# The triangle contraction taken by output side, with the moments, the next weight fold and the first normalization moved inside it, and contraction and finish in one block

## The chip, the cores and the metric

One core of one Trainium2 chip. The metric is device time in microseconds; the median of three runs is compared. The profile is one execution of the whole program.

## The reference

Four residual layers are applied in turn to an image `x` of 256 x 256 tokens with 64 channels. Each layer is a group normalization of x, followed by a "triangle multiplication":

```python
def layer(x):                       # x: (256, 256, 64), float32; weights differ per layer
    z  = layernorm(groupnorm(x))    # statistics of groupnorm run over the whole image
    a  = (z @ Wa + ba) * sigmoid(z @ Wag + bag)      # layers 0 and 2: also * mask
    b  = (z @ Wb + bb) * sigmoid(z @ Wbg + bbg)
    o  = einsum('ikc,jkc->ijc', a, b)                # layers 1 and 3: 'kic,kjc->ijc'
    g  = sigmoid(z @ Wog + bog)
    return x + ((layernorm(o) * g) @ Wo + bo         # layers 0 and 1: gate first
                if gate_first else (layernorm(o) @ Wo + bo) * g)   # layers 2 and 3
```

Layer 0 rounds a and b to bfloat16 before the contraction; the other layers contract in float32.

## The kernel before

Each layer runs through the same stages, one after the other.

- `prepare`: a few tiny operations that turn the statistics of x into the group normalization. It is a block of its own (a block ends with a barrier of all engines).
- One block with `norm` (x is normalized, split into two float16 parts and stored to DRAM as XH or XHA), and then, for each half of the channels, `project` (the four projections and gates, into the SBUF tensor LR) and `contract` (32 channel matrices of 256 x 256). `moments` closes this block.
- `finish`: a block of its own. It loads the contraction's result O, the normalized x (XH) and x itself (XT), and computes layer normalization, gate, output projection and residual.

**The contraction** of one half is 16 steps e; a step is four channels, eight float32 matmuls of 128 x 256 (each in two instructions), into one of four pairs of PSUM banks. Four steps are a *piece*: piece = (channel quarter cq, output side ut), with `cq, ut = divmod(piece, 2)`. So both output sides (rows 0 to 127 and 128 to 255 of the result) become complete only with the last pieces. ACT copies a step from PSUM to `obuf` (L879) and squares it (L885). DVE adds copy and squares into running sums `sum1`, `sum2` (four adds, L903 and L911). SP stores each piece to the DRAM tensor OS (OSL, in bfloat16, in layer 0); a store is 2 MB, 1 MB in layer 0.

**Moments** come after the last sum: DVE folds the two parts of the sums (L987 to L996), ACT takes logarithm and exponential (L1006, L1008) for 1/sqrt(variance). In layers 0 to 2 `fold(number + 1)` runs between these: it folds the next layer's normalization weights into its projection, with matmuls on PE (L331 to L341), one `Abs` on ACT and some fifteen small operations on DVE, in a chain of waits between the three.

**Finish** works on 16 chunks (4 rounds i of 4 buffers h), each of 4 tiles k, software-pipelined. A chunk takes three loads of 1 MB in all (O: two DMAs, half the size in layer 0; XH: two; XT: one) and one store of 1 MB. For a chunk DVE subtracts the mean (L1217) and POOL multiplies (L1186) in layers 0 and 1; in layers 2 and 3 DVE does one multiplication (L1225). For a tile PE transposes (L1105), projects the gate (L1117) and projects out (L1125), and in layer 3 transposes back (L1134). All four buffers of a chunk's loads are in LR, the tensor that the contraction reads, so a load may start only when the contraction has finished with that part of LR. All these loads and stores are issued by SP, in the order of its program:

```python
if half == 1 and piece >= 2:
    sp.wait_ge(contracted.s, contracted.n + 8)
    for h in (0, 1) if piece == 2 else () if low else (2,):
        load_xh(sp, layer, 0, h)
        load_xt(sp, layer, 0, h)
```

The quarter cq 0 is contracted by steps 0 to 7, so its part of LR is free after 8 of 16 steps, and XH and XT of chunks 0 and 1 (in slots 8, 9, 12, 13, 0, 1 of LR, a slot being 2048 columns) are loaded from there. `next_inputs` and `next_x` issue the loads of a round once their buffers have been used: O after the chunk has been centered, XH after its gates, XT after the chunk's sum, and then its store.

Of the kernel before, what the change touches and what calls it, by code (L numbers as in the profile page):

```python
# [48 lines left out]
P = 128  # L49
N = 256  # L50
# [53 lines left out]
def build(nc, x_in, masks, consts, params, out):  # L104
    ctx = ExitStack()
    with ctx:
# [112 lines left out]
        summed_up = sem("summed_up")  # L219
        normalized = sem("normalized")  # L220
# [96 lines left out]
        def fold(number):  # L317
# [8 lines left out]
            wfold, blast, wout_w = squares[0][0:C, 0:320], squares[0][0:C, 320:448], squares[0][:, 448:576]  # L326
            wproj, magnitudes = squares[1][:, 0:320], squares[1][:, 320:640]

            def on_pe(pe):
                pe.wait_ge(folded.s, folded.n + (3 if late else 2))  # L330
                pe.matmul(bank(3)[:, 0:320], K(K_DROP, C), wfold, start=True, stop=False)  # L331
                pe.matmul(bank(3)[:, 0:320], blast, w_cat, start=False, stop=False)
                pe.matmul(bank(3)[:, 0:320], K(K_LAST, 1), prm[0:1, W_BIAS:W_BIAS + 320],
                          start=False, stop=True).then_inc(weights.s, 1)
                if late:
                    pe.matmul(bank(6)[:, 0:P], K(K_CENTER_OUT), wout_w, start=True, stop=True)
                    pe.matmul(bank(7)[:, 0:1], w_out, vec(V_OB), start=True, stop=True).then_inc(late_folded.s, 1)
                pe.wait_ge(weights.s, weights.n + 4)
                pe.transpose(bank(4)[0:1, 0:P], most, K(K_IDENT)).then_inc(weights.s, 1)
                pe.wait_ge(weights.s, weights.n + 6)  # L340
                pe.matmul(bank(5)[:, 0:1], ones1[0:1, :], small[0:1, 9:10], start=True, stop=True) \  # L341
                    .then_inc(weights.s, 1)
# [11 lines left out]
            def copy(dve):  # L354
                dve.wait_ge(weights.s, weights.n + 1)
                dve.tensor_copy(wproj, bank(3)[:, 0:320]).then_inc(weights.s, 1)
# [5 lines left out]
            def rest(dve):  # L362
                if late:
                    dve.wait_ge(late_folded.s, late_folded.n + 1)
                    dve.tensor_copy(wout_c[:, :], bank(6)[:, 0:P]).then_inc(late_folded.s, 1)
                    dve.tensor_tensor(bias_c, bank(7)[:, 0:1], vec(V_BO), ALU.add).then_inc(late_folded.s, 1)
                dve.wait_ge(weights.s, weights.n + 5)
                dve.reduce_max(small[0:1, 9:10], bank(4)[0:1, 0:P], mybir.AxisListType.X).then_inc(weights.s, 1)
                dve.wait_ge(weights.s, weights.n + 7)
                dve.tensor_scalar(most, bank(5)[:, 0:1], 1e-30, 1.0 / W_SCALE, ALU.max, ALU.mult) \  # L370
# [18 lines left out]
            return on_pe, on_act, start, copy, greatest, rest  # L389
# [984 lines left out]
```

## Time and profile before

| | |
|---|---|
| median of 3 runs | 2281.32 us (2278.84 to 2282.44) |
| profiled execution, its time | 2283.2 us |
| its span, first to last instruction | 2281.3 us |
| PE busy | 1972.7 us (86%) |
| DVE busy | 1766.1 us (77%) |
| ACT busy | 1654.8 us (73%) |
| moved by DMA | 624.77 MB, 274 GB/s over the span |
| contraction of half 1 ends on PE, layers 1, 2, 3 | 998.4, 1565.2, 2102.3 us |
| first PE instruction of the finish, layers 0 to 3 | 485.8, 1021.1, 1583.5, 2119.4 us |

The granted TensorE clock of the execution was 0.941 of full. "Idle before <- name" in a row tells how long the engine stood still before it, and who ended that. DMA share is the mean busy share of the core's 16 DMA engines; it can show a little over 1.

### The profile page before, as it was taken

The numbers are of one execution on the slowest core, as the hardware profiler recorded it, in microseconds if no ns is written. First come the engines' busy times: TensorE is split into PE (matmuls) and PEld (weight loads), VectorE is DVE, ScalarE is ACT, GpSimd is POOL, SyncE is SP. The second block draws the span as 40 slices with busy tenths as digits, with TensorE's granted clock in tenths as the row PEclk, the third lists the DMA queues.
The fourth block names the chain that finished last, engine by engine and source line by source line (L and its number), as shares of the span: only waits on it lengthen the run. The fifth ranks groups of instructions, "written<-read, shape, count | busy, mean of one in ns | idle before, by whom it ended". The sixth has DMA issues, their size and how long they took to land. (4 is left out here: it accounts for less than half of the span.)

```text
span 2281.3 us, 48887 instructions
## 1 busy us (share of the span) xinstructions
PE 1972.7 (86%) x13892; PEld 1408.9 (62%) x13892; DVE 1766.1 (77%) x2907; ACT 1654.8 (73%) x2597; POOL 605.9 (27%) x564
## 2 busy tenths in 40 slices
PE   4599887759899898969889899897988989898898
PEld 3433767636433788955443498885553359797565
DVE  5678899979768887869758897877985888787554
ACT  2388788859878877749878785765655878585566
POOL 0000546435310000015420080640652000000575
PEclk8699988969999999989999999998998999999899
DMA  8879949579979837498969993939997985667996
GB/s 323 322 226 271 278 114 272 159 256 416 373 218 280 298 126 266 152 350 352 420 253 283 268 248 107 281 100 375 392 421 243 281 295 166 225 218 261 370 420 276
DMA packets 484453, 624.77 MB, mean 274 GB/s; under 512 B 16496, under 2 KB 376944, under 8 KB 467952
## 3 DMA queue, kind: packets, MB, share of 16 engines
q1 hardware_dynamic: 482032, 606.61, 78.1%
q10 hardware_dynamic: 2304, 16.78, 1.8%
q8 instruction: 52, 0.85, 0.2%
q14 instruction: 65, 0.53, 0.1%
HBM read 413.61 MB, written 209.72 MB: 273 GB/s over the span
## 5 line engine op out<-in xcount | busy, mean ns | idle before, releaser
L733 PE MATMUL bank<-whigh,obuf 128*128 128x128 f16 x4096 | 507.2, 227 | 66.0 <-DMA obuf<-XH 28.6
L733 PEld LDWEIGHTS bank<-whigh,obuf 128*128 128x128 f16 x4096 | 466.4, 125 | 72.1 <-issue 55.3
L733 PE MATMUL bank<-wlow,obuf 128*128 128x128 f16 x4096 | 506.4, 227 | 0.4 <-issue 0.4
L733 PEld LDWEIGHTS bank<-wlow,obuf 128*128 128x128 f16 x4096 | 467.0, 125 | 1.6 <-issue 1.6
L867 PE MATMUL bank<-LR 128*128 128x256 f32 (+1 forms) x1792 | 375.5, 372 | 32.8 <-ACT obuf L879 16.9
L867 PEld LDWEIGHTS bank<-LR 128*128 128x128 f32 (+1 forms) x1792 | 320.3, 180 | 86.3 <-ACT obuf L879 23.4
L1186 POOL TENSOR_TENSOR LR<-LR,sum 128x2048 f32<-128x2048 f32 x32 | 145.7, 4552 | 550.9 <-DVE LR L1217 550.9
L755 ACT ACTIVATE sigs<-bank,small 128x256 f32<-128x256 f32 x512 | 238.1, 475 | 63.1 <-PE bank L733 56.0
L603 PE MATMUL bank<-LR,cen 128*128 128x512 f32 x512 | 256.4, 626 | 22.4 <-DMA LR<-XT 11.2
L655 DVE SCALAR_TENSOR_TENSOR LR<-bank,small,LR 126x1024 f32<-126x1024 f32 x128 | 164.3, 1284 | 121.0 <-ACT LR L636 120.6
L755 ACT ACTIVATE squares<-bank,small 128x256 f32<-128x256 f32 x512 | 237.4, 475 | 14.6 <-PE bank L733 8.1
L879 ACT ACTIVATE obuf<-bank 128x1024 f32<-128x1024 f32 (+1 forms) x128 | 130.5, 1019 | 160.5 <-PE bank L867 143.5
L611 PE MATMUL bank<-LR,kst 128*128 128x512 f32 x512 | 240.9, 593 | 5.2 <-ACT LR L632 5.2
L1105 PEld LDWEIGHTS bank<-kst,LR 128*128 128x128 f32 x1024 | 151.8, 193 | 135.4 <-issue 72.6
L903 DVE TENSOR_TENSOR sum<-sum,obuf 128x512 f32<-128x512 f32 x256 | 175.6, 686 | 71.3 <-ACT obuf L879 71.3
L770 POOL TENSOR_TENSOR msgs<-sigs,mask_sb 128x256 f32<-128x256 f32 x192 | 126.8, 674 | 377.1 <-ACT sigs L755 370.2
L798 DVE SCALAR_TENSOR_TENSOR LR<-bank,small,squares 128x256 f32 x512 | 222.8, 477 | 3.4 <-ACT squares L755 2.5
L1199 POOL TENSOR_TENSOR LR<-LR 128x512 f32<-128x512 f32 x64 | 102.6, 1612 | 433.1 <-DVE LR L1251 432.9
L1117 PE MATMUL bank<-LR,wog 128*128 128x512 f16 x768 | 212.0, 386 | 0.0
L911 DVE TENSOR_TENSOR sum<-sum,squares 128x512 f32<-128x512 f32 x256 | 176.0, 688 | 38.7 <-ACT squares L885 38.7
L603 PEld LDWEIGHTS bank<-LR,cen 128*128 128x128 f32 x512 | 94.1, 197 | 172.1 <-issue 84.8
L1105 PE MATMUL bank<-kst,LR 128*128 128x128 f32 x1024 | 160.6, 280 | 42.6 <-DVE LR L1225 22.3
(128 smaller groups left out, 3229.8 us busy)
## 6 DMA issues: line engine op xcount, KB each, us to landing
LR<-XT SPq DMA_DIRECT2D x128, 512.0 KB, 5.1
obuf<-XH SPq DMA_DIRECT2D x128, 512.0 KB, 6.2
LR<-XT SPq DMA_DIRECT2D x64, 1024.0 KB, 12.9
obuf<-XHA SPq DMA_DIRECT2D x128, 512.0 KB, 4.6
XT<-obuf SPq DMA_DIRECT2D x48, 1024.0 KB, 15.6
OS<-obuf SPq DMA_DIRECT2D x24, 2048.0 KB, 8.4
LR<-OS SPq DMA_DIRECT2D x96, 512.0 KB, 11.7
LR<-XH SPq DMA_DIRECT2D x64, 512.0 KB, 11.0
```

The costliest lines, as they stand in the source:

```text
L603: last = pe.matmul(banks[t % 3][:, u * BANK:(u + 1) * BANK], cen[:, :], cols, start=True, stop=True)
L611: last = pe.matmul(banks[3][:, u * BANK:(u + 1) * BANK], K(K_MEAN), sq[t % 2][:, u * BANK:(u + 1) * BANK], start=True, stop=True)
L655: dve.scalar_tensor_tensor(yc[t % 4][0:kept, :], banks[t % 3][0:kept, :], cb[0:kept, :], rs[t % 4][0:kept, :], ALU.add, ALU.mult).then_inc ...
L733: last = pe.matmul(bank(g)[:, j * P:(j + 1) * P], tokens, w[:, half * P:(half + 1) * P], start=part == 0, stop=part == 1)
L755: act.activation(sig[g], bank(g).rearrange("p (m c) -> p c m", m=4)[:, C:, :], ACT.Sigmoid, scale=unscale).then_inc(gates_ready.s, 1)
L798: dve.scalar_tensor_tensor(dest[:, kt, :, bass.ds(m, 4)], bank(g).rearrange("p (m c) -> p c m", m=4)[:, 0:C, :], unscale, gate[g], ALU.mul ...
L867: last = pe.matmul(banks[e % 4][:, c * N:(c + 1) * N], src[:, kt, off_a + ch, ut * P:(ut + 1) * P], src[:, kt, off_b + ch, :], start=kt == ...
L903: dve.tensor_tensor(sum1[:, ut, :].rearrange("p (c v r) -> p c v r", c=2, r=16), sum1[:, ut, :].rearrange("p (c v r) -> p c v r", c=2, r=1 ...
L911: dve.tensor_tensor(sum2[:, ut, :], sum2[:, ut, :], squares[e % 2][:, 2 * two * N:2 * (two + 1) * N], ALU.add).then_inc(summed.s, 1)
L1105: last = pe.transpose(by_token(turn_bank(k))[:, :, j, :], n_t[h % len(nrm)][:, :, 4 * q + j], K(K_IDENT))
L1117: last = pe.matmul(bank(2 + k % 2), wog[w][:, :], pair_cols(x, q) if k_is_b else by_b(x, q), start=(w, part) == (0, 0), stop=w == 1)
L1186: pool.tensor_tensor(n_v[h], n_v[h], token(sum2, i, h), ALU.mult).then_inc(normalized.s, 1)
```

## The change

1. The pieces are ordered by output side: `ut, cq = divmod(piece, 2)`. Rows 0 to 127 of the result are complete after step 7 of half 1.
2. Three pairs of PSUM banks rotate instead of four; banks 6 and 7 serve the fold.
3. In half 1 the work of `moments` is placed between the steps. `fold` of the next layer is split into pieces: on PE before steps 4, 7 and 9, on DVE before steps 1, 4, 6, 8 and 10, on ACT before step 6. The moments of side 0 are taken before DVE's sums of step 9, their roots before ACT's step 12. Before DVE's sums of step 14 comes the first operation of the finish on chunk 0 (centering or multiplication).
4. `finish` is in the same block as the contraction; the barrier is gone. The moments of side 1 are taken in the finish, on DVE and ACT at tile 10 of round 0, and ACT loads the logarithm's table for it and the sigmoid's again.
5. Slots move: XT of the four buffers in 8, 12, 2, 3 (before 8, 12, 0, 2), XH in 9, 13, 6, 7 (9, 13, 1, 3), O in 4, 5, 10, 11 (4 to 7; layer 0 10, 11, 4, 5), the normalized chunks in 0, 1, 14, 15 or so. The transfers have the same shapes and sizes. SP's order changes, as shown.

```diff
-                    cq, ut = divmod(piece, 2)
+                    ut, cq = divmod(piece, 2)
...
-                    if e >= 4:
-                        pe.wait_ge(copied.s, copied.n + e - 3)
+                    if folds and e == 4:
+                        fold_project(pe)
+                    if folds and e == 7:
+                        fold_turn(pe)
+                    if folds and e == 9:
+                        fold_spread(pe)
+                    if e >= 3:
+                        pe.wait_ge(copied.s, copied.n + e - 2)
...
+                    if half == 1 and e == 9:
+                        dve.wait_ge(summed.s, summed.n + 36)
+                        moments(dve, 0)
+                    if half == 1 and e == 14:
+                        first, from_ = wide(fin_nrm(layer)[0]), wide(fin_os(layer)[0])
+                        dve.wait_ge(landed[0].s, landed[0].n + 32)
...
-                    if half == 1 and piece >= 2:
-
-                        sp.wait_ge(contracted.s, contracted.n + 8)
-                        for h in (0, 1) if piece == 2 else () if low else (2,):
-                            load_xh(sp, layer, 0, h)
+                    if half == 1 and piece == 2:
+
+                        for h in range(2):
+                            sp.wait_ge(stored[h].s, stored[h].n + 16)
+                        if not low:
+                            sp.wait_ge(contracted.s, contracted.n + 12)
+                        load_os(sp, layer, 0, 0)
+                        load_xh(sp, layer, 0, 0)
+                    if half == 1 and piece == 3:
+                        load_os(sp, layer, 0, 1)
+                        load_xh(sp, layer, 0, 1)
+                        for h in range(2):
                             load_xt(sp, layer, 0, h)
-                        if piece == 3:
-                            sp.wait_ge(stored[0].s, stored[0].n + 32)
-                            for h in (0,) if low else (0, 1):
-                                load_os(sp, layer, 0, h)
                     sp.wait_ge(copied.s, copied.n + 4 * (piece + 1))
...
+                else:
+                    sp.wait_ge(contracted.s, contracted.n + 16)
+                    for h in range(2, 4):
+                        load_os(sp, layer, 0, h)
+                        load_xh(sp, layer, 0, h)
+                        load_xt(sp, layer, 0, h)
...
+                def rest_of_roots(i, k):
+                    if second_side(i, k):
+                        act.preload_act_table_set("natural_log_exp_and_others")
+                        root(act, 1)
+                        act.preload_act_table_set("sigmoid_and_others")
```

## Rows read from the trace of the kernel before

**Rows 1.** The page: busy time and instructions of each engine.

```profile
PE 1972.7 (86%) x13892; PEld 1408.9 (62%) x13892; DVE 1766.1 (77%) x2907; ACT 1654.8 (73%) x2597; POOL 605.9 (27%) x564
```

**Rows 2.** Timeline of PE: ends of three contractions, the fold, first turns.

```profile
983.78 14.62 PE L867 MATMUL bank<-LR 128*128 128x256 f32 x67
...
1003.31 1.06 PE L331 MATMUL bank<-squares,kst 64*128 64x320 f32 x2 [4.90 <-DVE squares L352]
...
1005.36 1.43 PE L333 MATMUL bank<-prm,kst 1*128 1x320 f32 x2
...
1009.28 0.37 PE L339 MATMUL bank<-kst,small 128*1 128x128 f32 x1 [1.55 <-DVE small L360]
1010.79 0.58 PE L341 MATMUL bank<-small,ones 1*128 1x1 f32 x2 [1.14 <-DVE small L368]
1021.08 1.12 PE L1105 MATMUL bank<-kst,LR 128*128 128x128 f32 x4 [9.70 <-POOL LR L1186]
...
1508.01 57.21 PE L867 MATMUL bank<-LR 128*128 128x256 f32 x256 [2.79 <-DVE LR L798]
...
2083.75 18.51 PE L867 MATMUL bank<-LR 128*128 128x256 f32 x85
2119.44 1.12 PE L1105 MATMUL bank<-kst,LR 128*128 128x128 f32 x4 [17.18 <-DVE LR L1225]
```

**Rows 3.** Timeline of ACT, layer 1: last copies, table load of the finish.

```profile
994.99 1.02 ACT L879 ACTIVATE obuf<-bank 128x1024 f32<-128x1024 f32 x1 [1.34 <-PE bank L867]
...
998.44 1.02 ACT L879 ACTIVATE obuf<-bank 128x1024 f32<-128x1024 f32 x1 [1.34 <-PE bank L867]
...
1014.01 1.28 ACT L1178 ACT_TABLE_LOAD   x1 [2.31 <-PEq L1283]
```

**Rows 4.** Timeline of DVE: last sums, chunk 2 of layer 0, the last chunks.

```profile
465.83 0.68 DVE L911 TENSOR_TENSOR sum<-sum,squares 128x512 f32<-128x512 f32 x1
...
492.92 2.29 DVE L1217 TENSOR_TENSOR LR<-LR,sum 128x2048 f32<-128x2048 bf16 x1 [3.21 <-POOL LR L1186]
...
596.42 2.29 DVE L1217 TENSOR_TENSOR LR<-LR,sum 128x2048 f32<-128x2048 bf16 x1 [1.18 <-DMA LR<-OSL]
...
1001.79 0.69 DVE L911 TENSOR_TENSOR sum<-sum,squares 128x512 f32<-128x512 f32 x1
...
1143.50 2.29 DVE L1217 TENSOR_TENSOR LR<-LR,sum 128x2048 f32<-128x2048 f32 x1 [2.38 <-DMA LR<-OS]
...
1704.76 2.29 DVE L1225 TENSOR_TENSOR LR<-LR,sum 128x2048 f32<-128x2048 f32 x1 [2.45 <-DMA LR<-OS]
...
2251.77 2.28 DVE L1225 TENSOR_TENSOR LR<-LR,sum 128x2048 f32<-128x2048 f32 x1
```

**Rows 5.** Timeline of SP: first finish loads of layers 1 to 3, last OS.

```profile
972.30 2.00 SPq L840 DMA_DIRECT2D LR<-XHA  x1
...
1539.10 1.97 SPq L837 DMA_DIRECT2D LR<-XH  x1
...
2076.15 1.97 SPq L840 DMA_DIRECT2D LR<-XHA  x1
...
2227.19 0.88 SPq L828 DMA_DIRECT2D LR<-OS  x2
```

**Rows 6.** Busy by window; last columns: granted clock, DMA share, GB/s.

```profile
480.00:510.00 30.00, 23.52 (x101) 14.42 (x102) 20.82 (x29) 18.27 (x33) 18.14 (x4) 0.81 0.57 201
...
1020.00:1050.00 30.00, 27.14 (x123) 16.65 (x124) 23.93 (x38) 22.69 (x41) 19.13 (x5) 0.93 0.69 254
1100.00:1140.00 40.00, 32.08 (x145) 18.76 (x144) 29.73 (x53) 31.62 (x65) 18.08 (x5) 1.00 1.02 420
...
1590.00:1610.00 20.00, 19.84 (x93) 11.99 (x91) 17.67 (x21) 12.84 (x20) 14.53 (x10) 1.00 0.86 309
...
2121.00:2141.00 20.00, 20.00 (x99) 12.72 (x98) 10.06 (x10) 12.47 (x22) 12.03 (x7) 0.94 0.85 314
```

**Rows 7.** DMA issues, 2227 to 2229 us: count, KB each, median us to landing.

```profile
LR<-OS SPq DMA_DIRECT2D x2, 512.0 KB, 13.1
```

More of the change, by code:

```diff
@@ L219, in build @@
         summed_up = sem("summed_up")
+        moment = sem("moment")
         normalized = sem("normalized")
@@ L387, in rest @@
                                       ALU.mult).then_inc(weights.s, 1)
-            return on_pe, on_act, start, copy, greatest, rest
+            return project_pe, turn_pe, spread_pe, on_act, start, copy, greatest, row, rest
         def advance_fold(number):
@@ L856, in contract @@
             parts = [(piece, g) for piece in range(4) for g in range(4)]
+            folds = half == 1 and number + 1 < len(LAYERS)
+            if folds:
+                fold_project, fold_turn, fold_spread, fold_act, fold_start, fold_copy, fold_greatest, fold_row, fold_rest = \
+                    fold(number + 1)
             @block.tensor
@@ L916, in _ @@
             def _(sp):
-                if half == 1 and number + 1 < len(LAYERS):
+                if folds:
                     load_parameters(sp, number + 1)
                 for piece in range(4):
-                    cq, ut = divmod(piece, 2)
+                    ut, cq = divmod(piece, 2)
                     if half == 0 and piece == 3:
@@ L1013, in finish, with moments @@
-        def finish(number, layer):
+        def moments(dve, ut):
+            s1, t1, s2 = sum1[:, ut, 0:N], sum1[:, ut, N:2 * N], sum2[:, ut, 0:N]
+            n = moment.n + 8 * ut
+            dve.tensor_tensor(s1, s1, t1, ALU.add).then_inc(moment.s, 1)
+            dve.tensor_tensor(s2, s2, sum2[:, ut, N:2 * N], ALU.add).then_inc(moment.s, 1)
+            dve.wait_ge(moment.s, n + 1)
+            dve.tensor_scalar(s1, s1, 1.0 / C, None, ALU.mult).then_inc(moment.s, 1)
+            dve.wait_ge(moment.s, n + 3)
+            dve.tensor_tensor(t1, s1, s1, ALU.mult).then_inc(moment.s, 1)
+            dve.wait_ge(moment.s, n + 4)
+            dve.scalar_tensor_tensor(s2, s2, 1.0 / C, t1, ALU.mult, ALU.subtract).then_inc(moment.s, 1)
+            dve.wait_ge(moment.s, n + 5)
+            dve.tensor_scalar(s2, s2, 0.0, None, ALU.max).then_inc(moment.s, 1)
@@ L1074, in next_x @@
                         sp.wait_ge(x_ready.s, x_ready.n + 16 * i + 4 * h + 4)
                         sp.sem_inc(tick.s, 1)
-                        load_xt(sp, layer, i + 1, h)
-                        store(i, h)
-                    sp.wait_ge(stored[1].s, stored[1].n)
-                    pipeline(sp, rounds - 1, 4, (next_inputs, 0), (next_x, 1))
-                    if not end:
-                        for h in range(4):
-                            sp.wait_ge(stored[h].s, stored[h].n + 48)
-                        for h in range(2):
-                            sp.wait_ge(consumed.s, consumed.n + 4 * (rounds - 1) + h + 1)
-                            load_xt_chunk(sp, h, h, LAYERS[number + 1]["k_is_b"])
@@ new lines, in _ @@
+                for h in range(2):
+                    sp.wait_ge(stored[h].s, stored[h].n)
+                pipeline(sp, rounds - 1, 4, (next_inputs, 0), (next_x, 1))
+                if not end:
+                    for h in range(4):
+                        sp.wait_ge(stored[h].s, stored[h].n + 48)
+                    for h in range(2):
+                        sp.wait_ge(consumed.s, consumed.n + 4 * (rounds - 1) + h + (3 if low else 1))
+                        load_xt_chunk(sp, h, h, LAYERS[number + 1]["k_is_b"])
@@ L1272, in finish @@
                     (gate_ready, 4 * NCH), (gated_ready, 4 * NCH), (x_ready, 4 * NCH), (normalized, NCH))
+            advance((moment, 16))
             if gate_first:
@@ L1287, in build @@
                     contract(block, number, layer, half)
-                moments(block, number, layer)
-            finish(number, layer)
+                finish(block, number, layer)
 def constants():
```

557 lines of the change are left out of this document (286 added, 271 removed).

## The prediction

> **What bounds the kernel.** The page comes first: PE is busiest, at 86% [rows 1], so no engine bounds the whole, and the question is what stands still where the change works. That is the seam between contraction and finish, once in each of four layers. The timeline of PE shows its size: in layer 1 the contraction ends at 983.78 + 14.62 = 998.4, the fold runs from 1003.3 to 1011.4, and the first transpose of the finish starts at 1021.1 [rows 2]. So PE does nothing of its main work for 22.7 us in layer 1, and for 17.2 in layer 3, where there is no fold [rows 2]. That is the prize.
>
> The second view is the busy windows, and it spoils the prize. Once the finish is under way, the DMA engines are at share 1.02 and 420 GB/s, and PE is busy only 32.08 of 40 us [rows 6]. The DVE timeline says the same from the other side: the last chunk of layers 0, 1 and 2 waits 1.2, 2.4 and 2.5 us for the landing of O [rows 4]. A chunk moves 4.19 MB, 10.0 us at 420 GB/s. The finish of layers 1 and 2 ends when the transfers let it. The reader should see that for these layers the time is counted on the DMA queue, not on PE.
>
> **A ledger of that queue.** SP issues everything in one fixed order. From the moment the store of piece 1 is through until O of chunk 15 lands, the same transfers are served in every float32 layer. SP issued that store just before the first loads, at 972.3, 1539.1 and 2076.2 [rows 5]; 2.1 MB at 420 GB/s take 5.0 us, so it is through at 977.3, 1544.1 and 2081.2. O of chunk 15 arrives at 1143.5 and 1704.8 where DVE waits for it [rows 4]; in layer 3 it was issued at 2227.2, the second of the pair some 0.4 later, and took 13.1, so it was there at 2240.7 [rows 5, 7]. In between, the queue stood empty for 30 x 0.31 = 9.3 us in layer 1, 20 x 0.14 = 2.8 in layer 2 and 20 x 0.15 = 3.0 in layer 3 [rows 6]. What is left is 156.9, 157.9 and 156.5 us of transfer work. Three layers that agree within 1.4 us tell me that this is work and not waiting, and the change leaves these transfers alone.
>
> **What the change does to the queue.** Before, the first finish loads need eight steps, since cq 0 is then free. By output side, cq 0 is read again in piece 2, so they need twelve. A step takes 998.44 - 994.99 = 3.45 us [rows 3]. So the first load starts 4 x 3.45 = 13.8 us before the end of the contraction instead of some 26, and the queue is empty in between. From then on it should not run dry: 16.8 MB (two piece stores, four chunks) are issued in 14 us and need 40. I take 1.0 us for the start of an empty queue, half of SP's 2.0 for its first load [rows 5].
>
> **What it does to the contraction.** The fold moves onto PE's float32 stream (layers 1 and 2). The three 320-column products and two small ones run from 1003.3 to about 1007.7, after a pause, at the lower clock [rows 2]; at full clock I take half, 2.2 us. Before step 7 PE waits for the greatest weight, which DVE takes only after the sums of step 5; DVE's last sum ends 1001.79 + 0.61 - 998.40 = 4.0 after the contraction [rows 2, 4], so at step 7 PE has waited 4.0 - 3.45 = 0.55, plus DVE's half microsecond and the transpose (0.37 [rows 2], less at full clock): 1.4. Before step 9 likewise, with three DVE operations: 1.8. Sum 5.4 us, between 2.2 (no waits) and 10 (the full price of the rows, and a step lost). What queues behind is the contraction and with it the first loads. Three pairs of banks instead of four cost nothing: a copy takes 1.02 of 3.45 us [rows 3]. The fold, moments and first normalization on DVE lie in its idle time there. What hides in the finish: on ACT two table loads of 1.28 [rows 3] and two short roots, 3.4 us, and 2.2 us on DVE. In layers 1 and 2 the queue covers them, in layer 3 ACT's slack under PE does; in layer 0, with ACT nearly as busy as PE, they cost.
>
> The Trainium skill (Perfetto Trace Analysis, Matmul Optimizations) asks for all eight PSUM banks, and by it six of them should slow the contraction; the copy's row gives no price to that. Its page DMA: Bandwidth & Descriptors (Rules for kernel authors) says to issue a DMA early and wait late; the change issues these loads later, and the ledger is what that costs here.
>
> **The layers.**
>
> Layer 1: the queue resumes at 998.4 - 13.8 + 5.4 + 1.0 = 991.0, was free from 977.3, and no longer loses 9.3: 991.0 - 977.3 - 9.3 = +4.4.
>
> Layer 2: 1508.01 + 57.21 = 1565.2 is the old end [rows 2]; 1565.2 - 13.8 + 5.4 + 1.0 = 1557.8, less 1544.1 and 2.8: +10.9. It had almost no idle to win back, so it loses most.
>
> Layer 3: the end is at 2102.3 [rows 2], no fold; 2102.3 - 13.8 + 1.0 = 2089.5, less 2081.2 and 3.0: O of chunk 15 lands 5.3 later, at 2246.0. Before, it lay ready until DVE took it at 2251.8 [rows 4]; now compute is early and waits for it. 2246.0 - 2251.8 = -5.8. Without the queue this layer would win some 17: all of its gap [rows 2].
>
> Layer 0 contracts in bfloat16 and is bound by DVE, whose sums end at 466.4 [rows 4]. DVE now carries in between some 3.8 (fold), 2.2 (moments) and 2.3 (first centering), and waits 1.2 for PE at step 7: 476.0. Then centering of chunk 1 (2.3) and POOL's multiplication (4.6 with its start, as POOL's wait before chunk 2 repeats), so chunk 2 is centered at 483.2, not 492.9 [rows 4]: -9.7, and +3.4 for ACT: -6.3. Its queue resumes a few us later than before, since it waits for a store, and wins back some 8 of 12.9 idle us [rows 6], for -1 to -4. I take -4.
>
> Sum: -4 + 4.4 + 10.9 - 5.8 = +5.5. The profiled span of 2281.3 becomes 2286.8. Its own time was 2283.2, 1.9 above the span and above the median of 2281.3; on the median the forecast is 2287 us.
>
> **Rivals.**
>
> *The queue doesn't bind (2235).* If the share of 1.02 only mirrors demand, the seams vanish as meant: layer 0 -6.3; layer 1, chunk 2 centered 13.3 earlier, less 3.4, -9.9; layer 2 some -13; layer 3 -17. Together -46. For it: the idle seams are real. Against: PE starved at 420 GB/s for 40 us, and three equal ledgers.
>
> *Layer 3 keeps its gap (2273).* The landing of O in layer 3 rests on a median of two transfers. If it landed 10 us earlier than I think, layer 3 wins its 17, and layer 0 its 6.3: -6.3 + 4.4 + 10.9 - 17 = -8. This is the way to the other side; it decides if O of chunk 15 lands before 2240 after the change. For it: PE was busy without pause to the end there.
>
> *The inserted waits hold the float32 contraction longer (2297).* If each of PE's two waits costs a step of 3.45 rather than 1.6, or DVE at step 14 waits for O of chunk 0, the first loads shift by as much in layers 1 and 2: some +5 each. For it: DVE is in order, and its sums stand behind the fold. Against: it idles about a third of that stretch.
>
> **Chances.** The ledger 0.50 (2278 to 2295), the free queue 0.12, layer 3's gap 0.22, longer waits 0.16. The time is that of the ledger; the range, 2266 to 2298, takes in the second and most of the fourth and leaves out the first, and a little above. 0.2% is 4.6 us, about what a measurement can tell from no change. Faster: 0.12 + 0.18 + 0.04 = 0.34. Slower: 0.16 + 0.28 = 0.44. Within: 0.22.
>
> **What would show it.** The windows after: an empty queue for about 8 us before step 12, and then share 1.0 without the dip at the start of the finish. PE's first transpose within 1 us of the last contraction; PE with idle time before O of chunks 3 to 15, more than now, in layer 3 too. The span from the first load to O of chunk 15 near 157 us. The contraction of half 1 some 5 us longer in layers 1 and 2, not in 3. I am wrong if that span shrinks, if the queue is fed before step 12, or if DVE doesn't wait for O in layer 3.

## The result and the profile after

The changed kernel took 2290.81 us (median of 8 runs, 2286.90 to 2295.54), the kernel before 2282.49 beside it (8 runs, 2278.84 to 2287.90): a ratio of 1.0034 [1.0023, 1.0046]. The forecast was 2287, slower at 0.44. The profiled execution took 2290.19 us, with a span of 2288.4; its clock was 0.944.

PE does the same instructions and is busy for 7.4 us longer; layer 3 below shows how the same matmuls can take longer. The page's line, against [rows 1]:

```profile
PE 1980.1 (87%) x13892; PEld 1405.2 (61%) x13892; DVE 1774.6 (78%) x2931; ACT 1666.0 (73%) x2613; POOL 608.4 (27%) x564
```

**A measure by layer.** From ACT's first copy of half 1 to the first table load of the next layer's `prepare` (in layer 3, to the end of the span) lies all that the change touches. For layer 1, in the timeline of ACT of the kernel before:

```profile
946.64 1.02 ACT L879 ACTIVATE obuf<-bank 128x1024 f32<-128x1024 f32 x1 [4.44 <-PE bank L867]
...
1169.16 1.28 ACT L516 ACT_TABLE_LOAD   x1 [0.27 <-PEq L1049]
```

and of the kernel after:

```profile
945.64 1.02 ACT L914 ACTIVATE obuf<-bank 128x1024 f32<-128x1024 f32 x1 [3.14 <-PE bank L896]
...
1170.10 1.28 ACT L528 ACT_TABLE_LOAD   x1 [0.27 <-PEq L1350]
```

That is 222.5 and 224.5 us. I call it the *seam stretch*. Where two kernels have the same code in it, their profiles differ by 0.1 to 1.6 us, once by 3.5; so a difference of 1.6 us or less in the tables is not told apart from none. The stretches ahead of it vary by up to 5 us in a layer, though all that differs there between the kernels is the order and the banks of half 0's contraction, and this takes 34.0 us (layer 0) or 51.8 us in each of them. So a seam stretch says more of an edit than a span does. In the tables, in us:

| seam stretch | layer 0 | layer 1 | layer 2 | layer 3 | sum |
|---|---|---|---|---|---|
| before | 195.7 | 222.5 | 213.3 | 230.8 | 862.3 |
| after | 198.4 | 224.5 | 221.4 | 230.0 | 874.3 |
| difference | +2.7 | +2.0 | +8.1 | -0.8 | +12.0 |
| forecast | -4 | +4.4 | +10.9 | -5.8 | +5.5 |

The stretches lost 12.0 us, more than twice the 5.5 forecast. The rest of the span gives back 4.9 us in these two profiles (3.7 by the medians), where the change alters little more than the order and banks of half 0's contraction. So the total fell near its forecast partly by luck: layers 0 and 3 gave none of their 9.8 us, and two smaller misses and that rest made up for it.

**The contraction after** (timeline of PE, layer 1; then layer 3, against [rows 2]):

```profile
958.36 10.61 PE L896 MATMUL bank<-LR 128*128 128x256 f32 x48
970.04 0.27 PE L345 MATMUL bank<-kst,small 128*1 128x128 f32 x1 [1.07 <-DVE small L367]
970.15 7.07 PE L896 MATMUL bank<-LR 128*128 128x256 f32 x32
978.35 0.38 PE L349 MATMUL bank<-small,ones 1*128 1x1 f32 x2 [1.13 <-DVE small L375]
978.66 24.44 PE L896 MATMUL bank<-LR 128*128 128x256 f32 x112
1007.69 1.09 PE L1149 MATMUL bank<-kst,LR 128*128 128x128 f32 x4 [4.60 <-POOL LR L1244]
...
2114.38 1.09 PE L1149 MATMUL bank<-kst,LR 128*128 128x128 f32 x4 [2.02 <-ACT sigs L1198]
...
2132.38 2.05 PE L1169 MATMUL bank<-sigs,wout_c 128*128 128x512 f32 x2 [6.76 <-DVE LR L1312]
...
2151.37 0.69 PE L1149 MATMUL bank<-kst,LR 128*128 128x128 f32 x4 [2.56 <-ACT squares L1198]
```

The seam did close: 4.6 us in layer 1, where there were 22.7, and less than half a microsecond in layers 2 and 3. The two waits for the fold are 1.07 and 1.13 us. But PE stops again a few tiles on, above all for 6.76 us in layer 3.

**The queue after.** First loads on SP, in layers 1, 2 and 3, against [rows 5]:

```profile
989.38 0.83 SPq L847 DMA_DIRECT2D LR<-OS  x2
...
1558.40 0.83 SPq L847 DMA_DIRECT2D LR<-OS  x2
...
2096.45 0.83 SPq L847 DMA_DIRECT2D LR<-OS  x2
```

DVE's waits for O: chunk 15 of layers 1 and 2, then chunks 2 and 15 of layer 3, against [rows 4]:

```profile
1144.43 2.29 DVE L1277 TENSOR_TENSOR LR<-LR,sum 128x2048 f32<-128x2048 f32 x1 [0.56 <-DMA LR<-OS]
...
1714.26 2.29 DVE L1286 TENSOR_TENSOR LR<-LR,sum 128x2048 f32<-128x2048 f32 x1 [0.90 <-DMA LR<-OS]
...
2129.28 2.29 DVE L1286 TENSOR_TENSOR LR<-LR,sum 128x2048 f32<-128x2048 f32 x1 [8.31 <-DMA LR<-OS]
...
2258.85 2.28 DVE L1286 TENSOR_TENSOR LR<-LR,sum 128x2048 f32<-128x2048 f32 x1
```

Busy by window; the last columns are granted clock, DMA share and GB/s, as in [rows 6]:

```profile
980.00:990.00 10.00, 10.00 (x49) 8.79 (x48) 9.36 (x25) 4.84 (x5) 0.00 (x0) 1.00 0.21 68
990.00:1000.00 10.00, 10.00 (x48) 8.81 (x47) 8.41 (x14) 6.70 (x9) 0.00 (x0) 1.00 0.92 292
...
1550.00:1560.00 10.00, 10.00 (x48) 8.81 (x47) 9.35 (x24) 5.79 (x6) 0.00 (x0) 1.00 0.16 44
...
2110.00:2150.00 40.00, 30.03 (x133) 18.40 (x131) 22.14 (x28) 21.14 (x33) 14.16 (x10) 0.83 1.03 412
2110.00:2288.40 178.40, 160.83 (x833) 104.70 (x831) 90.71 (x93) 113.79 (x199) 100.80 (x64) 0.94 0.93 378
```

and of the kernel before, from the end of layer 3's contraction to the end:

```profile
2102.00:2281.30 179.30, 155.91 (x834) 102.81 (x832) 91.90 (x93) 113.03 (x198) 102.62 (x64) 0.94 0.89 358
```

The reader should see the hole before step 12 (share 0.21 and 0.16), the full queue behind it, and the time from the first load to O of chunk 15: 1144.43 - 989.38 = 155.0 us in layer 1 and 1714.26 - 1558.40 = 155.9 in layer 2. In layer 3 DVE doesn't wait for chunk 15 but for chunk 2, and in those first 40 us PE has 30.03 us of work, at clock 0.83.

The last two rows account for layer 3. Before, PE stood 17.2 us at the seam and then no more until the last tiles. After, it stands 2.02 + 6.76 + 2.56 = 11.3 us in three places, which is 5.8 less, and its same matmuls take 160.8 us instead of 155.9, which is 4.9 more: behind each stop they run slowly for a while (the pair behind the long one took 2.05 us, in full flow it takes 1.02). 5.8 won and 4.9 lost leave 0.9.

**Layer 0 after** (timelines of POOL, DVE and ACT):

```profile
467.25 9.09 POOL L1244 TENSOR_TENSOR LR<-LR,sum 128x2048 f32<-128x2048 f32 x1 [47.91 <-DVE LR L955]
478.85 4.54 POOL L1244 TENSOR_TENSOR LR<-LR,sum 128x2048 f32<-128x2048 f32 x1 [2.50 <-DVE LR L1277]
```

```profile
487.59 3.13 DVE L1025 TENSOR_TENSOR sum<-sum 128x256 f32<-128x256 f32 x1
490.64 0.41 DVE L1026 TENSOR_TENSOR sum<-sum 128x256 f32<-128x256 f32 x1
...
507.30 2.29 DVE L1277 TENSOR_TENSOR LR<-LR,sum 128x2048 f32<-128x2048 bf16 x1 [2.66 <-ACT sum L1043]
```

```profile
504.45 1.28 ACT L1227 ACT_TABLE_LOAD   x1
505.75 0.51 ACT L1041 ACTIVATE sum<-sum,epso 128x256 f32<-128x256 f32 x1
506.29 0.42 ACT L1043 ACTIVATE sum<-sum 128x256 f32<-128x256 f32 x1
506.72 1.28 ACT L1229 ACT_TABLE_LOAD   x1
```

### The profile page after: what moved, and what is told of

The parts are those of the page before. It is cut to its first block and busy times, and to the rows that moved or that the text cites. A ratio compares the mean times of both kernels' runs of the same rounds, so it can differ in the third digit from the quotient of the medians.

```text
span 2288.4 us, 48967 instructions
## 1 busy us (share of the span) xinstructions
PE 1980.1 (87%) x13892; PEld 1405.2 (61%) x13892; DVE 1774.6 (78%) x2931; ACT 1666.0 (73%) x2613; POOL 608.4 (27%) x564
## 5 line engine op out<-in xcount | busy, mean ns | idle before, releaser
L745 PE MATMUL bank<-whigh,obuf 128*128 128x128 f16 x4096 | 503.4, 226 | 63.6 <-DMA obuf<-XH 28.1
L1244 POOL TENSOR_TENSOR LR<-LR,sum 128x2048 f32<-128x2048 f32 x32 | 150.5, 4704 | 551.2 <-DVE LR L955 419.2
```

Source lines behind the costliest of these rows:

```text
L745: last = pe.matmul(bank(g)[:, j * P:(j + 1) * P], tokens, w[:, half * P:(half + 1) * P], start=part == 0, stop=part == 1)
L1244: pool.tensor_tensor(n_v[h], n_v[h], token(sum2, i, h), ALU.mult).then_inc(normalized.s, 1)
```

## The experiments

Theory, after the result: in layers 1 and 2 the total of the queue from the first load on sets the end, so the start of the loads is what counts. Layer 3 is lost where the first chunks arrive. Layer 0 is lost to the second side's moments. The seam stretches of all kernels, with the ratio of each to the kernel before on its chip:

| kernel | layer 0 | layer 1 | layer 2 | layer 3 | sum | median, us | ratio |
|---|---|---|---|---|---|---|---|
| load12_before | 196.0 | 229.8 | 220.0 | 238.0 | 883.8 | 2302.27 | 1.0089 [1.0071, 1.0107] |
| three_banks | 195.5 | 223.6 | 213.6 | 230.7 | 863.4 | 2283.75 | 1.0002 [0.9991, 1.0014] |
| fold_late | 195.7 | 222.6 | 218.2 | 230.2 | 866.7 | 2285.15 | 1.0005 [0.9990, 1.0019] |
| load_at_10 | 196.8 | 218.0 | 213.8 | 223.9 | 852.5 | 2269.15 | 0.9946 [0.9929, 0.9963] |
| no_xt_before | 193.6 | 208.6 | 205.8 | 230.9 | 838.9 | 2258.17 | 0.9894 [0.9867, 0.9922] |
| no_xt_after | 197.1 | 210.7 | 205.5 | 230.5 | 843.8 | 2261.90 | 0.9899 [0.9874, 0.9925] |
| load_at_10_fold_late | 195.5 | 215.4 | 211.4 | 220.4 | 842.7 | 2261.91 | 0.9904 [0.9881, 0.9926] |
| chunk2_early | 196.8 | 224.6 | 219.5 | 226.2 | 867.1 | 2288.44 | 1.0013 [1.0001, 1.0025] |
| no_second_side | 191.2 | 224.7 | 220.5 | 225.9 | 862.3 | 2282.04 | 0.9992 [0.9982, 1.0001] |
| all_three_repairs | 196.9 | 215.5 | 211.4 | 220.0 | 843.8 | 2259.52 | 0.9887 [0.9868, 0.9906] |
| first_on_dve | 194.0 | 224.6 | 220.5 | 230.7 | 869.8 | 2288.61 | 1.0033 [1.0021, 1.0046] |
| four_repairs | 194.2 | 215.5 | 210.9 | 220.0 | 840.6 | 2254.77 | 0.9881 [0.9866, 0.9896] |

**1. The late loads alone, in the kernel before (load12_before).**

```diff
-                        sp.wait_ge(contracted.s, contracted.n + 8)
+                        sp.wait_ge(contracted.s, contracted.n + (8 if low else 12))
```

> The kernel before, with one number changed: in layers 1 to 3 the first finish loads wait for 12 contraction steps, not 8. If the late start of the transfer queue is what costs (my theory): layer 2 resumes the queue at 1552.4 instead of 1544.1 and has only 2.8 us of emptiness to win back, +5.5; layer 1 has 9.3 to win back, 0 to +2; layer 3 has 11 us of slack before O of its last chunk is used, 0; layer 0 is untouched. Sum +5 to +8 us. If the cost of the change lies in the fold's waits on PE or in the banks, and the queue would have caught up, this run is unchanged: within 2 us.

Measured: +7.3, +6.7 and +7.2 us in layers 1 to 3, +20 in all. The expectation missed: it is far more than the ledger gives, and alike in three layers whose ledgers differ. SP and ACT in layer 1:

```profile
1007.24 10.47 SPq L828 DMA_DIRECT2D LR<-OS  x4
...
1018.99 0.59 SPq L845 DMA_DIRECT2D LR<-XT  x1
```

```profile
1019.99 1.28 ACT L1178 ACT_TABLE_LOAD   x1 [9.09 <-PEq L1283]
```

SP stands 10.5 us in the issues to a full queue and is through at 1019.6; 0.4 later the barrier between the two blocks opens. In layer 1 of the kernel before it opens at 1014.0 [rows 3], and there another engine came last. SP was through at 1012.6, DVE with the fold at 1013.7 (timelines of SP and DVE):

```profile
1012.05 0.59 SPq L845 DMA_DIRECT2D LR<-XT  x1
```

```profile
1013.44 0.28 DVE L384 TENSOR_TENSOR wog<-wlow,kst 128x128 f16<-128x128 f16 x1
```

In layers 0 and 2 too the barrier before opened 0.3 us after the fold's last operation. In layer 3, without a fold, it was SP that came last; ACT had finished its root at 2111.6 (timelines of SP and ACT):

```profile
2115.99 0.59 SPq L845 DMA_DIRECT2D LR<-XT  x1
```

```profile
2116.99 1.28 ACT L1178 ACT_TABLE_LOAD   x1 [5.39 <-PEq L1283]
```

Against half 1's first copy (946.64 and 945.79) the barrier of layer 1 opens at 67.4 us before and at 74.2 here: 6.8 later, and the layer is 7.3 longer. In layer 3 it opens 7.2 later (66.5 and 73.7), and the layer is 7.2 longer. So the later loads put SP last at the barrier in all three float32 layers, and what waits for the barrier came later by as much. My sum had neither this wait nor its price. That layers 1 and 2 lose by the same path, and not by the queue's later start, is argued: there both came later together. The change took this barrier away, and its late loads, with the fold on top, cost layer 1 only 2.0 us.

**2. Three pairs of banks, in the kernel before (three_banks).**

```diff
-                    if e >= 4:
-                        pe.wait_ge(copied.s, copied.n + e - 3)
+                    if e >= 3:
+                        pe.wait_ge(copied.s, copied.n + e - 2)
...
-                            last = pe.matmul(banks[e % 4][:, c * N:(c + 1) * N],
+                            last = pe.matmul(banks[e % 3][:, c * N:(c + 1) * N],
```

> The kernel before with three pairs of PSUM banks in the contraction instead of four. Theory: a copy takes 1.0 of 3.45 us of a step, so nothing changes, within 1.5 us of 2282. Rival (fewer banks slow the contraction): eight contractions of 16 steps; a tenth of a microsecond per step would be +13 us.

It costs nothing that can be measured; the float32 contraction's 51.8 us from first to last copy stay 51.8.

**3. The fold's waits one step later on PE (fold_late), in the changed kernel.**

```diff
-                    if folds and e == 7:
+                    if folds and e == 8:
                         fold_turn(pe)
-                    if folds and e == 9:
+                    if folds and e == 10:
                         fold_spread(pe)
```

> The changed kernel, with the fold's second and third part on PE one step later (before steps 8 and 10, not 7 and 9), so that DVE has finished what PE needs. The trace after shows PE standing 1.07 and 1.13 us at these places in layer 1, and a little around them. Theory: the contraction of layers 1 and 2, and with it the first loads and the whole queue, come 2.2 to 3 us earlier in each: -4.5 to -6 us against the changed kernel, some 2285. Rival (the waits are hidden, only the twelve steps count): within 1 us of the changed kernel, 2291.

From first to last copy half 1 went from 57.5 to 55.1 us in layers 1 and 2, and the seam stretches became 1.9 and 3.2 us shorter; layer 3, without a fold, stayed. Layer 0, which folds too, became 2.7 shorter; its half 1 went from 42.0 to 40.6 us, and the rest may be spread. PE no longer waits at either place (timeline of PE, layer 1):

```profile
957.43 14.06 PE L896 MATMUL bank<-LR 128*128 128x256 f32 x64
971.33 0.27 PE L345 MATMUL bank<-kst,small 128*1 128x128 f32 x1
...
978.44 0.38 PE L349 MATMUL bank<-small,ones 1*128 1x1 f32 x2
```

The contraction is 2.4 us shorter, the loads start earlier by that, and layers 1 and 2 end earlier by about as much.

**4. Residuals and O of chunk 0 two steps earlier (load_at_10), in the changed kernel.**

```diff
                     if half == 1 and piece == 2:
+                        if not low:
+                            sp.wait_ge(contracted.s, contracted.n + 10)
+                            for h in range(2):
+                                load_xt(sp, layer, 0, h)
                         for h in range(2):
                             sp.wait_ge(stored[h].s, stored[h].n + 16)
+                        load_os(sp, layer, 0, 0)
                         if not low:
                             sp.wait_ge(contracted.s, contracted.n + 12)
-                        load_os(sp, layer, 0, 0)
                         load_xh(sp, layer, 0, 0)
...
-                        for h in range(2):
-                            load_xt(sp, layer, 0, h)
+                        if low:
+                            for h in range(2):
+                                load_xt(sp, layer, 0, h)
```

> The changed kernel; XT of chunks 0 and 1 lie in slots 8 and 12 and O of chunk 0 in slot 4, which hold channels 0 to 7 and are free after 10 steps. They are loaded from there, and only XH of chunk 0 waits for step 12. Same transfers, other order. Theory (the queue's empty time before step 12 is the loss): 6.9 us earlier start with 3 MB to move in it, so layers 1 and 2 win 5 to 6.9 each, layer 3 2 to 6.9 since PE waits early in its finish: -12 to -20 against the changed kernel, some 2275, faster than the kernel before. Rival (queue time is not what sets the end): within 2 us of the changed kernel.

The ratio fell from 1.0034 to 0.9946: some 20 us, and the kernel is now faster than before. All three float32 layers win alike, 6.5, 7.6 and 6.1 us, two steps of 3.45 being 6.9. In layer 1 the first load goes out at 981.98 and O of chunk 15 comes 155.5 us later:

```profile
981.98 0.83 SPq L864 DMA_DIRECT2D LR<-XT  x2
```

```profile
1137.48 2.29 DVE L1281 TENSOR_TENSOR LR<-LR,sum 128x2048 f32<-128x2048 f32 x1 [2.29 <-DMA LR<-OS]
```

This is the experiment that settles layers 1 and 2: the same transfers, 155.0, 155.5 and 155.9 us, and the start decides. In layer 3 the win came another way: PE's wait at chunk 2 fell from 6.76 to 2.00 us, and its matmuls from the last copy on took 159.3 us instead of 160.6.

**5 and 6. Fewer transfers in the rounds: both kernels without the XT loads of rounds 1 to 3 (no_xt_before, no_xt_after).** These chunks add the residual of an older chunk.

```diff
-                    load_xt(sp, layer, i + 1, h)
+                    sp.sem_inc(loaded_xt[h].s, 16)
```

> The kernel before, leaving out the loads of XT in rounds 1 to 3 of every finish (12 of 16 chunks; the residual is then added from old data). A chunk's traffic falls from 4.19 to 3.14 MB, 7.5 us at 420 GB/s, below PE's 7.85. Theory (the queue sets the end of the finish in layers 1 and 2): PE no longer starves there, layer 1 some 10 and layer 2 some 5 us shorter, so 2265 to 2270. Rival (the queue does not bind): within 3 us of 2282.

> The changed kernel with the same loads of XT left out. With the queue relieved, the early compute should show: by my sums for a free queue the change is worth -46 us against the kernel before, and a queue relieved only in rounds 1 to 3 still holds the start of the finish. Theory: this run is 20 to 40 us shorter than the kernel before with the same loads left out. Rival (the change costs on the engines, not on the queue): this run is as slow against its partner as the change is against the kernel before, +8 us.

The kernel before won 13.9 and 7.5 us in layers 1 and 2 and nothing in layer 3 (+0.1): the queue bounds two layers and not the last. That is more than the 10 and 5 expected, and with 2.2 us in layer 0 the time, 2258, came out below the 2265 to 2270 expected. The second expectation missed. With 12.6 MB less per layer the changed kernel is still no faster (3.5 and 2.1 us slower in layers 0 and 1, 0.3 and 0.4 faster in 2 and 3). The rival missed as well: over the four stretches the changed kernel is 4.9 us slower than its partner, where without the edit it was 12.0. What is gone is layer 2's 8.1 us; the losses of layers 0 and 1 stay. Relieving the later rounds doesn't free its early start, since the first chunks are issued together, from step 12 on, before any round. Layer 3 of no_xt_after, timeline of DVE:

```profile
2105.87 2.29 DVE L1286 TENSOR_TENSOR LR<-LR,sum 128x2048 f32<-128x2048 f32 x1 [8.75 <-DMA LR<-OS]
```

The wait for O of chunk 2 is as long as ever (8.31 in the changed kernel).

**7. Experiments 3 and 4 together (load_at_10_fold_late).** Both diffs, nothing else.

> The changed kernel with both repairs: first loads at 10 steps and the fold's parts on PE one step later. Theory: the two add, -17 to -25 against the changed kernel, 2266 to 2274, faster than both. Rival: if one makes the other useless, no more than the better of them.

They add in layers 1 and 2 (215.4 and 211.4), and the whole, 2261.9, came out below the 2266 to 2274 expected. Layer 3 is 3.5 us shorter than in experiment 4 with the same code there. In its trace PE's wait at chunk 2 is 0.22 us and not 2.00, and its matmuls take 157.5 us and not 159.3, which is 3.6 us together; why O of chunk 2 was there earlier stays open, and it may be the spread of single profiles.

**8. O of chunk 2 ahead of the last piece's store (chunk2_early), in the changed kernel.**

```diff
-                        for h in range(2):
-                            load_xt(sp, layer, 0, h)
+                        load_xt(sp, layer, 0, 0)
+                        if low:
+                            load_xt(sp, layer, 0, 1)
+                        if not low:
+                            sp.wait_ge(contracted.s, contracted.n + 16)
+                            load_os(sp, layer, 0, 2)
+                            load_xt(sp, layer, 0, 1)
                     sp.wait_ge(copied.s, copied.n + 4 * (piece + 1))
...
                     for h in range(2, 4):
-                        load_os(sp, layer, 0, h)
+                        if low or h == 3:
+                            load_os(sp, layer, 0, h)
```

> The changed kernel (2290.8 us) with one edit in the order of the float32 layers' first loads: O of chunk 2, and then the second residual, are issued ahead of the last piece's store instead of behind it, so O of chunk 2 lands one store and one residual earlier (3.1 MB, 7.5 us at 420 GB/s). The queue carries the same bytes in the same total time. If layers 1 and 2 are bound by the queue's total until O of chunk 15, they stay as they are within 1 us each, although DVE's wait for O of chunk 2 goes there too. Layer 3 lost 8.3 us where DVE waited for O of chunk 2 and was bound by TensorE from then on, so it ends 5 to 7 us earlier: 2284 to 2287 in all. If instead every layer loses its gain at the arrival of chunk 2 (the rival), all three float32 layers end 5 to 7 us earlier each: 2271 to 2277. If layer 3 were bound by the queue's total as forecast, nothing would change in any layer: 2290 to 2292.

By layer it went as the first theory said, in a smaller size: layer 3 -3.8 us, layer 1 +0.1. Layer 2 moved by -1.9, a little more than the 1 us allowed. DVE and PE, layer 3:

```profile
2127.43 3.01 DVE L1292 TENSOR_TENSOR LR<-LR,sum 128x2048 f32<-128x2048 f32 x1 [0.57 <-DMA LR<-OS]
```

```profile
2138.78 1.46 PE L1167 MATMUL bank<-LR,wog 128*128 128x512 f16 x3 [3.14 <-DMA LR<-XHA]
```

The wait for O shrank from 8.31 to 0.57, and 3.14 us of it came back for XH of the same chunk, which still stood behind the store: a full queue hands a wait on. The whole time moved by 0.0021 in the ratio, some 5 us, with intervals of 0.0012 on either side, so that it is only just clear of noise.

**9. Without the second side's moments (no_second_side), in the changed kernel.** The eight operations and two table loads of the second side are left out, so that half of the output is normalized with raw sums.

```diff
                     if second_side(i, k):
-                        moments(dve, 1)
+                        dve.sem_inc(moment.s, 6)
...
-                        act.preload_act_table_set("natural_log_exp_and_others")
-                        root(act, 1)
-                        act.preload_act_table_set("sigmoid_and_others")
+                        act.sem_inc(moment.s, 2)
```

> The changed kernel without the second output side's moments and roots, which it does inside the first round of every finish (six VectorE operations, two on ScalarE and two table loads; the numbers of the second half of the output are normalized with raw sums, so only its time counts). If what was lost of layer 0's early start is this insertion (some 5 us on DVE, one operation of it 3.13 us beside a multiplication of POOL, and 3.5 us on ScalarE), layer 0 ends 4 to 7 us earlier. Layers 1 and 2 are bound by the queue and stay within 1 us. Layer 3 is past its wait for the queue by then and bound by TensorE: 0 to 4 us earlier. Sum: 2280 to 2287. The rival, that these operations hide everywhere: within 1 us of 2290.8.

-7.2, +0.2, -0.9 and -4.1 us: the insertion costs where the transfers don't cover it, and nothing that can be told from the spread where they do. In layer 3 it was not a wait that went: PE's stop of 2.56 us is gone, but its wait at chunk 2 grew from 6.76 to 9.41, and what fell is the time of its matmuls from the last copy on, from 160.6 to 156.4 us. Layer 0 is now 4.5 us shorter than before. Chunks 3 and 4 of layer 0 are centered on time, 69.0 and 76.7 us after half 1's first copy, where the changed kernel does it at 73.4 and 85.7, first behind DVE's inserted operations and then behind ACT's:

```profile
495.49 2.29 DVE L1275 TENSOR_TENSOR LR<-LR,sum 128x2048 f32<-128x2048 bf16 x1 [0.23 <-POOL LR L1242]
503.17 2.29 DVE L1275 TENSOR_TENSOR LR<-LR,sum 128x2048 f32<-128x2048 bf16 x1
```

**10. Experiments 3, 4 and 8 together (all_three_repairs).** As experiment 7, with O of chunk 2 ahead of the store.

> Both repairs of before (the residuals of chunks 0 and 1 and O of chunk 0 loaded after ten and twelve steps, the fold's two waits on TensorE one step later) and O of chunk 2 ahead of the last piece's store. The two repairs gave 2261.9. Layer 3 there still waited 3.5 us for O of chunk 2 and was bound by TensorE after it; layers 1 and 2 are at the queue's pace. So only layer 3 gains, 2 to 4 us: 2258 to 2260. If the queue's total bounds layer 3 as well: 2262, no gain.

The expectation missed: layer 3 moved by -0.4 us against experiment 7 and not by 2 to 4. Layer 0, with the same code, moved by +1.4, layers 1 and 2 by 0.1 at most, and the intervals of 0.9887 and 0.9904 overlap. DVE's wait for chunk 2 in load_at_10 was 3.5 us, PE's behind it 2.0, and in experiment 7 PE's was 0.22 already. There was nothing left to win there.

**11 and 12. The first chunk's multiplication on DVE, in layers 0 and 1 (first_on_dve in the changed kernel, four_repairs on top of experiment 10).**

```diff
                             dve.tensor_tensor(first, from_, token(sum1, 0, 0), ALU.subtract).then_inc(mean_off.s, 1)
+                            dve.wait_ge(moment.s, moment.n + 8)
+                            dve.wait_ge(mean_off.s, mean_off.n + 1)
+                            dve.tensor_tensor(first, first, token(sum2, 0, 0), ALU.mult).then_inc(normalized.s, 1)
...
                 def normalize(i, h):
+                    if first(i, h):
+                        return
                     pool.wait_ge(mean_off.s, mean_off.n + 4 * i + h + 1)
```

> The changed kernel with one multiplication moved in layers 0 and 1: the first chunk's, which POOL does while DVE still sums, is done by DVE right behind the centering. In the changed kernel's trace this multiplication took 9.09 us on POOL in layer 0 beside DVE's sums (4.5 alone), and in layer 1 a sum of DVE took 5.00 us beside it instead of 0.69. If the two engines shut each other out there, DVE's own multiplication costs 2.3 us (its subtraction of the same shape took 2.29) and nothing is shut out: in layer 0 TensorE's first turn comes 5 to 7 us earlier against half 1's first copy and chunk 1 is centered 2 us earlier, so layer 0 ends 1 to 3 us earlier; in layer 1 DVE's sums end 2 us earlier, and the end stays within 1 us, since the queue sets it. In layers 2 and 3, within 1 us. Sum: 0 to 4 us below the changed kernel, 2287 to 2291. If there is no such shutting out and POOL's 9.09 us came from its own start, DVE loses 2.3 us in both layers and layer 0 ends 0 to 2 us later.

> The three repairs (2259.5, ratio 0.9887) and the first chunk's multiplication on DVE in layers 0 and 1. Layer 0 ends 1 to 3 us earlier; in layer 1 the transfers still set the end, within 1 us: 2256 to 2260. If the multiplication costs DVE 2.3 us and wins nothing: 2260 to 2263.

Timelines of DVE and PE in layer 0 of first_on_dve:

```profile
466.06 2.29 DVE L955 TENSOR_TENSOR LR<-LR,sum 128x2048 f32<-128x2048 bf16 x1
468.45 2.29 DVE L958 TENSOR_TENSOR LR<-LR,sum 128x2048 f32<-128x2048 f32 x1
```

```profile
471.00 1.09 PE L1152 MATMUL bank<-kst,LR 128*128 128x128 f32 x4 [13.42 <-DVE LR L958]
```

The multiplication takes 2.29 us on DVE, where POOL had needed 9.09. Against half 1's first copy (422.75 here, 421.58 in the changed kernel) PE's first turn comes at 48.3 instead of 55.0 us, and layer 0 ends 4.4 us earlier, in four_repairs 2.7 (the kernels with the changed kernel's layer 0 lie between 196.8 and 198.4, so part of the 4.4, which is more than the 1 to 3 expected, is spread). The whole time doesn't confirm it: 1.0033 against 1.0034, with intervals that leave room for 4 us either way. I hold the gain in the layer's stretch for shown and the gain in the whole for not shown. four_repairs, at 2254.77 us and 0.9881 [0.9866, 0.9896], is the fastest version that computes all, 27 us below the kernel before; all_three_repairs isn't told apart from it.

## Why the prediction held, and where its steps failed

**Right: the queue bounds layers 1 and 2.** The ledger forecast 156.9 and 157.9 us of transfer work; 155.0 and 155.9 were measured, and experiment 4 shows that the start alone moves the end. Experiments 5 and 6 show the bound from the other side. The first load was forecast 44.4 us after half 1's first copy (991.0 - 946.64) and came after 43.7 (that is SP's issue; the forecast had 1.0 for the start of the queue in it, so the split between start and work is not sharp). So the terms +4.4 and +10.9 became +2.0 and +8.1 because the work was 2 us less than the ledger had, and the start 0.7 sooner. The bytes explain some of the 2 us. Over the ledger's windows 63.7 and 63.6 MB moved before, and from the first load to O of chunk 15 63.1 and 63.5 after; at 407 GB/s that is 1.4 us in layer 1 and 0.5 in layer 2. The rest is open. The bound itself is not: from first load to O of chunk 15 it is 63 MB at 406 to 407 GB/s in the changed kernel and in experiment 4.

**Right: the fold on PE costs some 5.4 us.** From first to last copy half 1 grew from 51.8 to 57.5 us: 5.7. The waits were 1.07 and 1.13 where I had 1.4 and 1.8, so the matmuls and what stands around them took more than the 2.2 I gave them. The third rival, waits of a step each, fell with this. The banks are settled too: three pairs cost nothing that can be measured (experiment 2), where the Trainium skill (Perfetto Trace Analysis, Matmul Optimizations) asks for all eight; no run here shows a price for two fewer.

**Wrong in its place: layer 3.** The step was "Before, it lay ready until DVE took it at 2251.8; now compute is early and waits for it", -5.8 us. DVE took O of chunk 15 at 2258.85 without any wait. From the first load at 2096.45 the work of 155 us ends near 2251.5, so O lay ready some 7 us. The size of the term was near (counted from half 1's first copy, 193.1 us against 195.5 forecast); what was wrong is that this landing ends the layer. Layer 3 was held much earlier, at chunk 2: 8.31 us of DVE, 6.76 of PE, and two shorter stops of PE, 2.02 us behind ACT and 2.56 at the inserted table loads. And the sum had no term for the clock, which was 0.83 over the first 40 us: the same matmuls took 4.9 us more. After that PE was busy to the end, as before. The ledger counts what is through by the end; it doesn't say when chunk 2 is there, and chunk 2 stood behind the loads of two chunks and two stores. Experiments 4, 8 and 9 each took a part of it off: -6.1, -3.8 and -4.1 us. The second rival, that layer 3 keeps its whole gap, fell as well. Its sign, O of chunk 15 before 2240, did not come, but DVE never waited for that chunk, and yet the layer won only 0.8: the landing of chunk 15 was the wrong thing to decide by, for the forecast and for the rival.

**Wrong: layer 0.** The step was a lead of 9.7 us at chunk 2, less 3.4 for ACT. Against half 1's first copy chunk 2 was centered at 61.9 instead of 66.6 us, a lead of 4.6, since POOL's first multiplication took 9.09 us and not 4.6. Then the insertion cost 7.2 us (experiment 9) and not 3.4: DVE's own part, 5 us with one operation at 3.13 instead of 0.4, was charged only at 2.2 and then dropped, and both engines are in order, so that their costs follow one another: against experiment 9 chunk 3 is centered 4.4 us later and chunk 4 another 4.7. -4.6 + 7.2 = +2.6, and +2.7 was measured.

**Missing: what came last at the barrier.** What the gap before was made of I took as fold and moments. In layers 0 to 2 that was right: the barrier opened 0.3 us after the fold's last operation. In layer 3 some 5 us of the 17.2 were SP's issues to a full queue. It did not change the forecast's sum, but it made the expectation for experiment 1 too small by 12 us or more.

**Signs.** The hole before step 12, the full queue behind it and the span near 157 us came as forecast. PE's first turn came right behind the contraction in layers 2 and 3, but 4.6 us later in layer 1, where POOL's multiplication of chunk 0 began only 0.6 us before the contraction ended. In layer 3 PE's idle time came before chunk 2 and not before chunks 3 to 15.

**Open.** The 3.7 us by which the medians differ less than the seam stretches. In the two profiles PE was busy for 8.7 us less outside the stretches (1230.7 us against 1239.4) for the same instructions. Over all kernels no such gain is seen: the spans less the stretches are on average 1416.3 us in the four kernels with the old code and 1417.1 in the ten with the changed code, and with the medians in place of the profiled times it is the changed code that has some 1.6 us less.

## What to carry to other kernels

Where a full DMA queue bounds a stage, count its transfers from the first one on: in layers 1 and 2 here, closing a gap of the engines won nothing, and each microsecond by which the first transfer was later was lost whole. Two steps of earlier loads, on buffers that were free anyway, turned this change from 0.3% slower into 0.5% faster, and with the fold's waits moved to 1%. But a ledger only gives the end of the stage. For the start, list the order of issue and ask when each of the first inputs lands, since compute that was moved forward meets the transfers there. And an operation inserted into a running pipeline can cost the sum over its in-order engines, as in layer 0, unless some wait covers it. Last, a gap moved from the seam into the stage is not only idle time: count what the matmuls behind each stop lose by the clock.

## What the runs showed of the hardware

DVE and POOL can shut each other out. In layer 0 POOL's multiplication began at 467.25, while DVE ran eight sums without a pause until about 472.0, at their usual 0.69 us each; POOL was done 4.4 us after the last of them, the time that the operation takes alone (4.5). It got nothing in between. In layer 1 it was DVE that stood:

```profile
1002.39 0.68 DVE L964 TENSOR_TENSOR sum<-sum,obuf 128x512 f32<-128x512 f32 x1
1002.99 5.00 DVE L972 TENSOR_TENSOR sum<-sum,squares 128x512 f32<-128x512 f32 x1
```

beside a multiplication of POOL from 1002.55 to 1007.43. Not every operation of DVE stands. Beside POOL's multiplication from 485.89 to 490.44 in layer 0, this one, which reads PSUM (a bank), took its usual time, and the next but one, whose inputs both lie in SBUF, took the 3.13 us shown above instead of 0.41:

```profile
486.33 0.68 DVE L1293 TENSOR_TENSOR squares<-bank,squares 128x512 f32<-128x512 f32 x1
```

The Trainium skill (SBUF — State Buffer, SBUF: two separate sides) has this as an exclusive lock on a shared pair of ports, taken on DVE's side by operations with two SBUF inputs among others, that the loser waits out; the rows agree, and add that DVE's stream kept POOL out for several instructions in a row, not for one. Experiment 11 shows what avoiding it is worth: 6.8 us at PE's first turn.

SP's issue is not free when the queue is full: a group of four loads took 10.47 us of SP's time in experiment 1, and the barrier at the end of the block opened 0.4 us after SP's last issue. In layer 1 of the kernel before, two such groups followed each other: the first took 1.76 us, the second 10.39.
